# A two-layer transformer stack on one core: 72 identity products on a constant left out in the last third

## The chip, the core and the metric

One core of a Trainium2 chip. The time is the device time of one execution in microseconds (us). The engines are TensorE (PE: matrix products, with its weight loads shown as PEld), VectorE (DVE), ScalarE (ACT), GpSimd (POOL) and the DMA queues; SyncE (SP) issues most of the DMAs. Each engine works through its own list in order, and the lists wait for each other by semaphores.

## What is computed

Batch 2, 1024 tokens, 64 channels, f32. Five steps, each but the first added to its input and behind a layer norm:

```
h = W[x] + pe                                  # embedding and positions
h = h + linear_attention(layernorm(h))         # 8 heads, elu + 1
h = h + moe_block(layernorm(h))                # causal attention, then 8 experts, top 2
h = h + gated_toeplitz(layernorm(h))           # layer 1, the last third of the time
h = h + (layernorm(h) @ weight.T + bias)       # the end
```

The step in the last third, for x = layernorm(h) (the **third norm**):

```
u = silu(x @ u_w.T + u_b);  v = silu(x @ v_w.T + v_b)      # 192 columns each
out = irfft(rfft(a) * rfft(v))[:n]                         # a: a small network of the position
out = (u * out) @ o_w.T + o_b                              # output projection
x_r = silu(srms((x - out) @ t_w.T + t_b));  result = x + x_r
```

Then the **fourth norm** and the last projection (64 to 64 columns).

## The kernel before

All activations stay in SBUF: `h`, `xc`, `sq` and `x1` hold 8 tiles of 128 tokens by 2 x 64 channels (both batches side by side). The order of every engine is written out by hand, one function per engine. PSUM (`ps`) has 8 banks of 128 x 512 f32; which bank a step takes is fixed in the code.

A norm goes like this. DVE (`centre`, L1236) adds what the step before left in PSUM to `h` and subtracts the mean, in two halves; ACT squares each half (L983); DVE sums the squares (L1234) and forms the variance (L1245); ACT takes the root (L1143 for the third norm, L1186 for the fourth); DVE forms the reciprocal and scales the two halves (`scale_rows`, L1250), counting the semaphore `n3` or `n4` up by one for each. PE waits for that semaphore and transposes the tiles, four per half, by products with the identity `idt` (`transposes`, L506). ACT copies the first half to `xT`, DVE the second, and the next products read `xT`.

TensorE's list in the last third, in order:

- the last products of the experts (`last_experts_out`), which the third norm needs;
- `keep_warm(22, 6)` at L868;
- the transposes of the third norm (wait for `n3`);
- 8 steps `uv(n)` for v: four f32 products with 64 rows on `xT` and two bf16 products that add the bias, 192 columns each, and ACT's silu behind each step (L1160);
- the forward transform: 12 groups of 8 products on `tu_s`, with the 8 steps `uv` for u between them; DVE and POOL multiply and add;
- the inverse transform on `tk_s`, 4 units, with transposes (L921) and the two halves of the output projection;
- `keep_warm(4, 3)` at L953;
- the transposes of x - out (wait for `d3`, which DVE counts up at L1592 behind each half of the output projection), the products with `t3` (ACT copies one half of `xT`, L975, DVE the other, L1204);
- `keep_warm(46, 7)` at L957, while DVE and ACT work on srms, silu, the sum and the fourth norm;
- the transposes of the fourth norm (wait for `n4`) and the last projection; DVE adds it to `h` in two halves (L1619), each stored by one DMA.

`keep_warm(n, bank)` multiplies a constant, 128 x 512 in bf16, by the identity, n times:

```
def keep_warm(n, bank):
    for _ in range(n):
        mm(ps[:, bank], ident_b, bfc_s[:, 0:512])
```

Both operands lie in SBUF since the start. The products carry no wait and no semaphore, and nobody reads what they leave in the bank. Seven more calls stand earlier in the kernel; they aren't touched.

In the profile an f32 product is shown as two instructions, a bf16 product as one. The line of most products is L299, that of the helper `mm`.

Of the kernel before, what the change touches and what calls it, by code (L numbers as in the profile page):

```python
# [175 lines left out]
def build(nc, idx, emb, pe, wpack, rpack, epack, ident, bfc, rope, tm, tu, tk, out):  # L176
    with ExitStack() as ctx:
# [51 lines left out]
        def plan(region, *parts):  # L229
# [15 lines left out]

        qst, kst, yT, pt = plan(arena, ([2, B * NH, 512], BF16), ([B * NKV, N], BF16), ([4, 512], F32), ([PT_SLOTS, 2, 512], F32))
        _, _, _, pieces_q0, pieces_k, pieces_q1, e_raw = plan(
            arena, ([B * NH, N], BF16), ([B * NKV, N], BF16), ([4, 512], F32),
            ([NTERM, 512], BF16), ([NTERM, 512], BF16), ([NTERM, 512], BF16), ([NSPLIT], F32))
        pieces_q = (pieces_q0, pieces_q1)  # L250

        _, _, rope_s, tm_s = plan(arena, ([B * NH, N], BF16), ([B * NKV, N], BF16), ([2, N], F32), ([2, NM, L], F32))

        fhl, sil, gh, wb, zp_ = plan(arena, ([NT, B, P], F32), ([2, 512], F32), ([GSLOTS, 3, 512], F32),
# [3 lines left out]

        us, vs, osp, prd = plan(arena, ([NT, 384], F32), ([NT, 384], F32), ([NB * NK, 2, 384], F32), ([4, 2, 384], F32))
        _, yT3 = plan(arena, ([NT, 384], F32), ([NT, 3, P], F32))  # L260

        gt2 = sb("gt2", [P, P])
# [30 lines left out]
        def S(name):  # L293
            if name not in names:
                names[name] = sem(name)
            return names[name]

        def mm(o, l, r, start=True, stop=True, **kw):
            return nc.tensor.matmul(o, l, r, start=start, stop=stop, **kw)  # L299
# [200 lines left out]
        def _(pe):  # L500
            def transposes(src, banks, ready, done, values=(1, 2)):

                for j in range(NT):
                    if j % 4 == 0:
                        pe.wait_ge(ready, values[j // 4])
                    ins = nc.tensor.transpose(ps[:, banks + j // 4, (j % 4) * P:(j % 4 + 1) * P],  # L506
                                              src[:, j].rearrange("p b c -> p (b c)"), idt[:])
                    if j % 4 == 3:
                        ins.then_inc(done, 1)
# [10 lines left out]
# [4 lines that stand above are left out]
# [341 lines left out]
                    ins.then_inc(S("wT"), 1)  # L865
            last_experts_out()

            keep_warm(22, 6)  # L868
            transposes(x1, 2, S("n3"), S("T3"))


# [53 lines left out]
            def output_projection(blk):  # L925

                pe.wait_ge(S("yT3"), 2 * NU * (blk + 1))
                pe.wait_ge(S("uv_silu"), 2 * NT)
                for jj in range(4):
                    n = 2 * (2 * blk + jj - 2) if jj >= 2 else 2 * (2 * blk + 1 - jj) + 1  # L930
                    for c in range(3):
                        ins = mm(ps[:, 6 + blk, jj * P:(jj + 1) * P], yT3[:, n, c, :], W("o3", c * P, (c + 1) * P),
                                 start=(c == 0), stop=(c == 2))
                ins.then_inc(S("o3"), 1)
# [15 lines left out]
            output_projection(0)  # L950
            back_transposes(NB * NU - 1)
            output_projection(1)
            keep_warm(4, 3)  # L953
            transposes(xc, 4, S("d3"), S("T3b"))
            projection("xT3b", "t3", 0, S("t3"))

            keep_warm(46, 7)  # L957
            transposes(sq, 2, S("n4"), S("T4"))
            projection("xT4", "w4", 4, S("o4"))

# [830 lines left out]
```

## Time and profile before

| | before |
|---|---|
| median of 3 runs | 367.31 us (366.73 to 368.72) |
| the profiled execution | 368.48 us, of which the span in the profile 366.7 us |
| mean granted TensorE clock in it | 0.977 of 2.4 GHz |
| PE busy | 323.0 us (88%), 1703 products |
| DVE, ACT, POOL busy | 237.2, 144.1, 105.4 us |
| products with operands in `bfc_s` alone, from 256 us on | 72, 16.0 us busy, mean 379 ns |

The span is cut into 40 slices on the page; the line of PE's busy tenths shows 9 in nearly all slices behind the first eighth, and that of the granted clock 9 in nearly all of them. Three views carry the working: the chain of work that ended last in order of time (what released what), the timeline of a short stretch (what each engine did, with the idle time ahead of it and who ended it), and the table of stretches (busy time of each engine and the granted clock, 1.00 being 2.4 GHz and 0.50 being 1.2 GHz). An instruction's duration includes the time until its result has left the array, so products that follow each other closely overlap, and the sum of their durations is more than the time they take together.

### The profile page before, as it was taken

The page shows a single profiled execution, that of the slowest core. Times are in us where ns is not written, and L with a number is a line of the kernel's source. Part 1 is how long each engine was busy: PE and PEld are TensorE (multiplying, and loading weights), DVE is VectorE, ACT ScalarE, POOL GpSimd, SP SyncE. Part 2 cuts the span into 40 slices and gives each one's busy share as a digit, 9 for nine tenths or more (in the row PEclk, how much of TensorE's full clock was granted, in tenths as well). Part 3 has the DMA queues.
Part 4 walks back from the last instruction along what each step waited for, and adds up shares of the span by engine and source line. Part 5 has one row for each costly group of instructions (what it writes and reads, how often), then busy time and mean ns, then how long its engine had stood idle before and what let it go on. Part 6 is the DMA issues. An engine that isn't in the chain of part 4 may idle for free.

```text
span 366.7 us, 4601 instructions
## 1 busy us (share of the span) xinstructions
PE 323.0 (88%) x1703; PEld 180.6 (49%) x1703; DVE 237.2 (65%) x398; ACT 144.1 (39%) x238; POOL 105.4 (29%) x137
## 2 busy tenths in 40 slices
PE   1256988987999999979999999999999999899995
PEld 0122665552433434656754555555555555467734
DVE  0578678878998740357784555553856677745385
ACT  2022416460586686521554445553450120012250
POOL 5787000236321223200002422221004878700000
PEclk9997899999999999989899999999999999999998
DMA  7939500068000000000000000000000000000001
GB/s 257 321 103 419 216 2 0 0 118 143 2 3 0 4 2 1 2 0 2 0 1 2 0 0 3 0 0 2 1 2 0 0 2 0 0 0 3 0 0 59
DMA packets 6168, 15.29 MB, mean 42 GB/s; under 512 B 1282, under 2 KB 3714, under 8 KB 5506
## 3 DMA queue, kind: packets, MB, share of 16 engines
q1 hardware_dynamic: 5583, 14.45, 12.8%
q0 software_dynamic: 512, 0.53, 0.6%
q8 instruction: 14, 0.23, 0.3%
q14 instruction: 8, 0.07, 0.1%
q10 hardware_dynamic: 51, 0.01, 0.0%
HBM read 12.05 MB, written 0.52 MB: 34 GB/s over the span
## 4 chain that ended last, share of the span: by engine, by line
PE 66%; DVE 15%; ACT 6%; POOL 5%; issue 4%; DMA 2%; SPq 1%; DVEq 0%; POOLq 0%; ACTq 0%
PE ps L299 64%; POOL e_lo L426 2%; DVE arena L1485 1%; DMA idt<-ident 1%; DMA arena<-arena 1%; DVE share L1278 1%; DVE xc L1242 1%; DVE st L1234 1%; DVE st L1241 1%; DVE sq L1250 1%; POOL arena L492 1%; DVE rw L1416 1%; ACT L989 1%; PE ps L506 1%; ACT sq L983 1%
## 5 line engine op out<-in xcount | busy, mean ns | idle before, releaser
L1416 DVE TENSOR_REDUCE rw<-ps 128x1 f32<-128x512 f32 (+2 forms) x80 | 45.7, 629 | 7.6 <-PE ps L299 7.2
L299 PE MATMUL ps<-bfc_s 128*128 128x512 bf16 (+2 forms) x201 | 49.2, 358 | 0.0
L1102 ACT ACTIVATE arena<-ps 128x1024 f32<-128x1024 f32 (+3 forms) x48 | 37.6, 812 | 29.0 <-PE ps L299 28.6
L299 PE MATMUL ps<-arena 96*128 96x512 bf16 (+7 forms) x192 | 43.0, 328 | 1.4 <-DMA arena<-arena 0.8
L299 PE MATMUL ps<-xs,e_hi 128*128 128x512 f32 x96 | 40.6, 423 | 0.6 <-ACT arena L1128 0.6
L1485 DVE TENSOR_TENSOR arena<-ps,arena 128x512 f32<-128x512 f32 x48 | 33.1, 691 | 11.2 <-ACT arena L1128 10.8
L1128 ACT ACTIVATE arena<-ps 128x512 f32<-128x512 f32 x48 | 28.6, 597 | 26.3 <-PE ps L299 22.6
L299 PE MATMUL ps<-xs,e_lo 128*128 128x512 f32 x96 | 38.6, 402 | 0.0
L299 PE MATMUL ps<-share,tu_s 128*128 128x384 f32 x96 | 32.5, 488 | 0.0
L299 PEld LDWEIGHTS ps<-arena 96*128 96x128 bf16 (+1 forms) x192 | 15.8, 98 | 29.0 <-DVE rw L1416 13.2
L299 PEld LDWEIGHTS ps<-bfc_s 128*128 128x128 bf16 x201 | 20.2, 101 | 17.9 <-issue 2.5
L299 PE MATMUL ps<-w,xT 128*128 128x128 f32 (+3 forms) x160 | 26.7, 353 | 2.2 <-DVE xT L1448 0.8
L299 PEld LDWEIGHTS ps<-xs,e_hi 128*128 128x128 f32 x96 | 18.4, 191 | 16.3 <-ACT arena L1128 7.0
L299 PE MATMUL ps<-share,rp 128*128 128x256 f32 x14 | 8.0, 671 | 19.8 <-DVE share L1273 8.4
L299 PEld LDWEIGHTS ps<-w,xT 128*128 128x128 f32 (+1 forms) x160 | 20.0, 210 | 9.5 <-issue 4.8
L458 POOL TENSOR_SCALAR_AFFINE_SELECT arena<-arena 128x256 f32<-128x256 f32 (+1 forms) x32 | 13.8, 433 | 37.1 <-ACT arena L1102 36.6
L299 PE MATMUL ps<-arena,ew 64*64 64x512 f32 (+1 forms) x128 | 24.2, 610 | 0.0
L1264 DVE TENSOR_TENSOR arena<-ps,arena 128x512 f32<-128x512 f32 x16 | 10.3, 687 | 21.0 <-PE ps L299 21.0
L299 PE MATMUL ps<-arena,tk_s 128*128 128x384 f32 x64 | 21.4, 488 | 1.8 <-DVE arena L1555 1.8
L299 PEld LDWEIGHTS ps<-share,tu_s 128*128 128x128 f32 x96 | 17.6, 190 | 10.6
L299 PE MATMUL ps<-arena,va 128*32 128x512 f32 (+3 forms) x192 | 21.6, 505 | 0.7 <-ACT arena L1089 0.5
L299 PEld LDWEIGHTS ps<-xs,e_lo 128*128 128x128 f32 x96 | 18.5, 193 | 2.5
(237 smaller groups left out, 491.5 us busy)
## 6 DMA issues: line engine op xcount, KB each, us to landing
arena<-arena SPq DMA_DIRECT2D x24, 96.0 KB, 2.8
w<-wpack SPq DMA_DIRECT2D x1, 2152.5 KB
arena<-tm SPq DMA_DIRECT2D x2, 1024.0 KB, 5.8
arena<-epack SPq DMA_DIRECT2D x1, 1540.0 KB, 11.4
arena<-rope SPq DMA_DIRECT2D x1, 1024.0 KB
tu_s<-tu SPq DMA_DIRECT2D x2, 512.0 KB, 12.4
tk_s<-tk SPq DMA_DIRECT2D x2, 512.0 KB, 13.9
rp<-rpack SPq DMA_DIRECT2D x1, 678.5 KB, 4.5
```

The costliest lines, as they stand in the source:

```text
L299: return nc.tensor.matmul(o, l, r, start=start, stop=stop, **kw)
L426: nc.gpsimd.tensor_tensor(e_lo[:, 0:E_CUT], e_raw[:, 0:E_CUT], e_hi[:, 0:E_CUT].bitcast(F32), ALU.subtract).then_inc(S("e_split"), 1)
L458: nc.gpsimd.affine_select(out=v, in_=v, pattern=[[0, 2], [1, P + behind]], compare_op=ALU.is_ge, fill=0.0, base=-behind, channel_multiplie ...
L492: nc.gpsimd.tensor_tensor(dst[:, 0], p1[:, 0], p1[:, 1], ALU.subtract).then_inc(S("part"), 1)
L506: ins = nc.tensor.transpose(ps[:, banks + j // 4, (j % 4) * P:(j % 4 + 1) * P], src[:, j].rearrange("p b c -> p (b c)"), idt[:])
L983: nc.scalar.activation(sq[:, 4 * a:4 * a + 4], src[:, 4 * a:4 * a + 4], ACT.Square).then_inc(S("squared"), 1)
L989: nc.scalar.activation(unused[:, loads[0]:loads[0] + 1], idt[0:1, 0:1], func)
L1102: nc.scalar.activation(pt[:, n % PT_SLOTS, :, lo:512], ps[:, bank:bank + 2, lo:512], ACT.Exp, scale=HD ** -0.5).then_inc(S("exp_done"), 1)
L1128: nc.scalar.activation(sil[:, m % 2], ps[:, m % 2], ACT.Silu).then_inc(S("silu"), 1)
L1264: V.tensor_tensor(zp_[:, n % 2], ps[:, 5 + n % 2], wb[:, n % 2], ALU.mult).then_inc(S("zpair"), 1)
L1416: V.tensor_reduce(top_view(m, part)[:, at:at + len(heads), i], src, AXX, ALU.max, negate=True).then_inc(S("ring_read"), 1)
L1485: V.tensor_tensor(gh[:, n % GSLOTS, n3], ps[:, 2 + m % 3], sil[:, m % 2], ALU.mult).then_inc(S("gated"), 1)
```

## The change

The three calls in TensorE's list behind the experts are left out: 22, 4 and 46 products, 72 in all. Nothing is added, no wait is changed, and no other engine's list is touched.

```diff
@@ -865,7 +865,6 @@
             last_experts_out()
 
-            keep_warm(22, 6)
             transposes(x1, 2, S("n3"), S("T3"))
@@ -950,11 +949,9 @@
             output_projection(1)
-            keep_warm(4, 3)
             transposes(xc, 4, S("d3"), S("T3b"))
             projection("xT3b", "t3", 0, S("t3"))
 
-            keep_warm(46, 7)
             transposes(sq, 2, S("n4"), S("T4"))
             projection("xT4", "w4", 4, S("o4"))
```

## Rows read from the trace of the kernel before

**Rows 1.** The page: busy time of PE, and the chain by engine.
```profile
PE 323.0 (88%) x1703; PEld 180.6 (49%) x1703; DVE 237.2 (65%) x398; ACT 144.1 (39%) x238; POOL 105.4 (29%) x137
...
PE 66%; DVE 15%; ACT 6%; POOL 5%; issue 4%; DMA 2%; SPq 1%; DVEq 0%; POOLq 0%; ACTq 0%
```

**Rows 2.** Chain in order, third norm: start us, us, what.
```profile
265.24 0.67 PE ps L506 x4
...
266.72 6.46 PE ps L299 x48
...
273.74 29.92 PE ps L299 x120
```

**Rows 3.** Timeline, third norm: start us, us, engine, line, operation, [idle before].
```profile
257.66 1.97 PE L299 MATMUL ps<-ew,arena 128*128 128x64 f32 x16
...
259.46 4.91 PE L299 MATMUL ps<-bfc_s 128*128 128x512 bf16 x22
...
265.24 1.26 PE L506 MATMUL ps<-idt,x 128*128 128x128 f32 x8 [0.86 <-DVE x L1250]
```

**Rows 4.** Chain piece, then timeline, around the output projection.
```profile
340.00 3.81 PE ps L299 x28
...
342.79 1.03 PE L299 MATMUL ps<-bfc_s 128*128 128x512 bf16 x4
342.99 0.69 DVE L1592 TENSOR_TENSOR xc<-xc,ps 128x512 f32<-128x512 f32 x1 [3.54 <-PE ps L299]
...
343.65 1.04 PE L506 MATMUL ps<-idt,xc 128*128 128x128 f32 x8
344.29 0.58 ACT L975 COPY xT<-ps 128x512 f32<-128x512 f32 x1 [4.33 <-PE ps L506]
344.72 0.69 DVE L1204 COPY xT<-ps 128x512 f32<-128x512 f32 x1 [1.05 <-PE ps L506]
...
344.93 2.05 PE L299 MATMUL ps<-w,xT 128*128 128x128 f32 x16 [0.24 <-ACT xT L975]
```

**Rows 5.** Timeline around the fourth norm and the last projection.
```profile
346.81 10.09 PE L299 MATMUL ps<-bfc_s 128*128 128x512 bf16 x46
...
358.85 1.26 PE L506 MATMUL ps<-idt,sq 128*128 128x128 f32 x8 [1.94 <-DVE sq L1250]
...
360.18 3.36 PE L299 MATMUL ps<-w,xT 128*128 128x128 f32 x16
```

**Rows 6.** Stretches, us: PE, PEld, DVE, ACT, POOL busy (x), PEclk, DMA, GB/s.
```profile
32.99:36.40 3.41, 2.58 (x6) 1.00 (x5) 2.88 (x4) 1.11 (x2) 1.90 (x3) 0.50 0.98 416
36.40:39.82 3.42, 3.42 (x8) 2.01 (x8) 1.57 (x3) 0.35 (x1) 0.00 (x0) 0.50 1.01 414
...
155.90:159.28 3.38, 1.68 (x14) 1.33 (x13) 1.50 (x5) 0.91 (x3) 0.00 (x0) 1.00 0.00 0
159.28:162.70 3.42, 3.28 (x12) 2.39 (x13) 1.25 (x3) 0.45 (x1) 0.00 (x0) 0.50 0.00 0
...
172.90:176.35 3.45, 3.45 (x28) 3.27 (x28) 0.95 (x3) 0.21 (x1) 0.00 (x0) 1.00 0.00 0
176.35:179.76 3.41, 2.99 (x8) 1.87 (x7) 2.59 (x8) 2.54 (x5) 0.00 (x0) 0.50 0.00 0
...
357.25:360.66 3.41, 1.74 (x12) 1.32 (x13) 2.31 (x6) 0.80 (x2) 0.00 (x0) 1.00 0.02 5
360.66:364.07 3.41, 2.88 (x15) 2.58 (x13) 2.49 (x4) 0.00 (x0) 0.00 (x0) 0.50 0.15 56
```

**Rows 7.** Timeline, PE alone: transposes, then products of 128 columns, low clock.
```profile
37.87 0.42 PE L544 MATMUL ps<-idt,share 128*128 128x128 f32 x1
38.08 0.42 PE L545 MATMUL ps<-idt,share 128*128 128x128 f32 x1
...
159.42 2.08 PE L299 MATMUL ps<-w,xT 128*128 128x128 f32 x8 [0.79 <-DVE xT L1448]
```

**Rows 8.** Timeline, PE alone: a long wait without a fall.
```profile
89.04 0.24 PE L299 MATMUL ps<-bfc_s,mpc 128*48 128x128 bf16 x1 [2.19 <-POOL mpc L446]
```

## The prediction

> **What bounds the kernel now.** I read the page first. PE is busy 323.0 of 366.7 us, and the chain that ended last lies on PE for 66% of the span [rows 1]; but a busy share counts the identity products too, so it can't say what they are worth. The chain in order of time can. Around each of the three places the reader should ask one thing: is the PE work there on the chain, or does the chain run over DVE and ACT while PE does something that nobody waits for?
>
> At the third norm (257 to 265 us) the chain runs through DVE and ACT: adding the experts' result, centring, squares, sums, root, scaling. It meets PE again only with the first transposes at 265.24, for 0.67 us, then the two ACT copies and 6.46 us of u and v products [rows 2]. The 22 products of L868 lie beside that, from 259.46 for 4.91 us, so they end at 264.37, before the scaled rows are there; PE then stands idle 0.86 us waiting for DVE [rows 3]. From 273.74 on the chain stays on PE, so what the u and v products lose isn't made up later [rows 2].
>
> At the output projection (340 to 347 us) the 4 products of L953 are on the chain: the piece at 340.00 has 28 products, 24 of the projection and 4 of the identity [rows 4].
>
> At the fourth norm (347 to 359 us) the chain is on DVE and ACT again, and the 46 products (10.09 us from 346.81, so to 356.90) lie beside it; PE then waits 1.94 us for DVE [rows 5].
>
> So two of the three groups cost nothing as work. What they do instead is keep TensorE occupied through 5.6 and 11.9 us in which it would stand still. The granted clock by stretch shows what standing still does here: 1.00 (2.4 GHz) nearly everywhere, 0.50 (1.2 GHz) in four low stretches, of 6.8 us (33 to 40, two rows), 3.4 us from 159.28, 3.4 us from 176.35 and 3.4 us from 360.66 [rows 6]. Ahead of the second and the last, PE was busy for only 1.68 and 1.74 us of the 3.4 us shown; ahead of the third it was full, and the clock fell nevertheless, so the busy share alone doesn't decide. The last one matters most: it came in spite of the 46 products, after 1.94 us of idleness and the transposes, and the final projection is run mostly in it.
>
> **First place (L868, 22 products).** As work: 0, it is hidden by the DVE and ACT work of the norm. That leaves PE idle from the end of the experts' last transposing products (257.66 + 1.97 = 259.63) to 265.24 [rows 3], 5.6 us. That is far more than the 1.94 us ahead of the last low stretch, so I take the clock to be at 1.2 GHz when the transposes start. Costs:
> - Four transposes on the chain. At full clock they take 0.67 us [rows 2]. At half clock one takes 0.42 us and the next starts 0.21 later (37.87 and 38.08) [rows 7]: 0.42 + 3 x 0.21 = 1.05, so +0.4. The other four are covered by the two ACT copies.
> - u and v products until the clock is back. The first eight steps are 48 products (each step 4 on `xT` in f32 and 2 bias products in bf16) in 6.46 us, 0.81 each, one piece of PE in the chain, so PE sets the pace [rows 2]. No row shows it at half clock. Nearest rows: the last projection's 128-column products, 16 in 2.05 us (0.128 each) at full clock [rows 4] against 15 begun or ended in 2.88 us (0.19; 0.23 from start to start below, in the third place) in the low stretch [rows 6], factors 1.5 and 1.8; the two levels give 2 at most. I take 1.75, since these products have more columns (192), and it is columns that the clock counts: each low microsecond loses 0.43. How long? The low stretches lasted 3.4 us where PE was dense and 6.8 us where the first half had holes [rows 6]. Here the front part is used up by idleness and transposes, so the u and v products see between 2.6 and 6 us of it; I take 4.5. Loss 2.0 us, with ends 2.6 x 0.33 = 0.9 and 6 x 0.5 = 3.0. All of it is on the chain.
>
> The Trainium skill (TensorE: Matmul & The Clock Gate, Part 1: The HAM clock gate) says that the array is throttled by default and that activity releases it, and puts the penalty at the throttled time times (1 - K/N). By it 4.5 us at half rate would cost 2.25 us where I take 2.0, an estimate from that page; it speaks against leaving the products out. Its section on PE-mode transpose adds that transposes don't count as busy in the same way; the last low stretch, which fell after eight of them, agrees.
>
> **Second place (L953, 4 products).** The first four transposes need the first half of DVE's subtraction, done at 339.45 (342.99 less the 3.54 that DVE was idle before the second half), so only the 4 products hold them to 343.65. Without these they can start about 342.8, right behind the projection, and the ACT copy about 343.4 instead of 344.29. The second four wait for 342.99 + 0.69 = 343.68 [rows 4]; they end some 0.7 later, the DVE copy at about 345.1 (344.72 + 0.69 = 345.41 before). The projection then starts at about 344.15, runs into that copy at 345.15 for its second half, and ends 1.03 later (8 of its 16 products), near 346.2 instead of 344.93 + 2.05 = 346.98. Gain 0.75 us; its ends are 0.5 and 1.03, the whole duration of the four. What is late next is the second half of the subtraction, hence not 1.03. PE is busy on both sides of this place, so the clock stays.
>
> **Third place (L957, 46 products).** As work: 0, hidden by the DVE and ACT work of the two norms. PE idles 11.9 us before the transposes, so they start at half clock: +0.4 as above. The final projection took 3.36 us for 16 [rows 5]; its first 4 were still at full clock. Entirely low: 8 such products took 2.08 us at 159.42, the last one's drain among it [rows 7]; less that drain some 1.85, 0.23 each from start to start, so 3.5 to 3.8 us: +0.3. Against an execution in which this projection is run at full clock (2.05 us [rows 4]) it is 1.6 instead of 0.3. DVE's and ACT's part isn't changed.
>
> **Sum.** 0.4 + 2.0 - 0.75 + 0.4 + 0.3 = +2.35 us. The profiled execution took 368.48 us (span 366.7 and 1.8 around it), so 370.8. The median of the runs shown is 367.31, 1.2 us less; the runs lie from 366.73 to 368.72. Added to the median, 369.7. But the place of a low stretch can vary between executions, and a median run may well have had its last projection at full clock; then the change costs 2.35 + 1.3 = 3.65 and gives 371.0. I take a value between them, nearer the first: **370.2 us**.
>
> **Rivals.**
> - The clock holds at the first place, or is back before the u and v products. For it: PE idled 2.19 us at 86.7 to 89.0 without the clock falling [rows 8]. Against it: 5.6 us is over twice that. Then -0.75 + 0.7 + up to 1.3: 367.3 to 368.6, not measurable.
> - The other side, faster or no slower: TensorE's clock costs nothing at the end because the granted level doesn't matter to transposes and small products, so only the four products on the chain count. It decides if the last projection's pitch of some 0.2 against 0.128 were not the clock's. Then 367.31 - 0.75 = 366.6. The two pitches at either level speak plainly against it.
> - The clock doesn't come back in the u and v stage. Those products use 64 rows of the array, and no row shows a low stretch ended by such work. The level would then return only in the transform behind 273.74 [rows 2]: 6.46 us of products lose 0.75 to 1.0 of their time, some 5.5 us, plus 1 us of the transform. 367.31 + 0.4 + 6.5 + 0.35 - 0.75 = 373.8.
> - That the change doesn't do what it says: the products write a bank nobody reads before it is overwritten, and no one waits on them; nothing here.
>
> **Chances.** Forecast, 368.7 to 371.8: 0.66. Clock holds or is back early: 0.19. Only the four count: 0.04. Late return: 0.11. The range takes in the forecast and half of either neighbour: 368.2 to 372.0. About 0.5% (1.8 us) is what a measurement of this kernel can tell from no change. Slower by more than that means over 369.15: most of the forecast (0.57) and the late return (0.11), 0.68. Faster by over 0.5% needs more than the four products can give: 0.03. The rest, 0.29, lies between.
>
> **What would show it.** In the profile after: granted clock 0.50 when the transposes at about 265 start and for 2.6 to 6 us of u and v products, whose pitch goes from 0.81 to about 1.4 us; the third-norm chain on DVE unchanged until 264.5; the stretch from the output projection's start (340.00 before) to the last t3 product shorter by 0.75; 0.50 over all of the last transposes and the projection, which takes 3.5 to 3.8 us. The prediction is wrong if the clock is at 1.00 in the u and v stage, if their pitch doesn't follow the clock, or if the low stretch there runs past 273.

## The result and the profile after

The changed kernel takes 375.62 us in the median of 4 runs (374.17 to 376.87), the kernel before 368.01 us (4 runs, 366.73 to 368.79). The ratio is 1.0214, with a 95% interval of 1.0177 to 1.0251: slower by some 7.9 us (7.6 between the two medians). The forecast was 370.2 and a range of 368.2 to 372.0: the direction was right, and the sum of +2.35 us was too small by a factor of more than three.

From the page of the profiled execution (376.05 us, span 374.3): busy time by engine, the granted clock in 40 slices, and the chain by engine.

```profile
PE 314.7 (84%) x1621; PEld 177.9 (48%) x1631; DVE 237.7 (63%) x398; ACT 144.1 (38%) x238; POOL 105.6 (28%) x137
...
PEclk9998999996999999998999999999557999999956
...
PE 66%; DVE 15%; ACT 5%; POOL 5%; issue 5%; DMA 2%; SPq 1%; DVEq 0%; POOLq 0%; ACTq 0%
```

PE is busy for 8.3 us less than in [rows 1], and the kernel takes 7.6 us more of span. The clock line has a hole of 5, 5, 7 in slices 29 to 31, and another near the end. PE's share of the chain is the same 66%: the time went into products that were on the chain anyway.

The 6 in slice 10 lies in code that is the same in both kernels, and up to 264 us the two executions are level within 0.3 us. It is worth a look even so, because it is the wait of [rows 8], 2.20 us here against 2.19 there. Timeline, then stretches (columns as in [rows 6]; the clock is the third number from the end):

```profile
87.45 0.30 PE L299 MATMUL ps<-bfc_s,mpc 128*48 128x128 bf16 x1 [2.20 <-POOL mpc L446]
```

```profile
87.00:90.50 3.50, 3.05 (x8) 1.15 (x9) 2.13 (x4) 0.00 (x0) 0.32 (x2) 0.51 0.57 101
90.50:93.90 3.40, 3.40 (x13) 1.62 (x12) 2.27 (x5) 0.00 (x0) 0.00 (x0) 0.50 0.00 0
```

In this execution the clock fell in that wait and was back at 93.9; in the profiled execution of the kernel before it didn't fall. So whether an idle stretch of 2.2 us costs the clock differs here between executions of the same code. The products that brought it back were dense, bf16, and on 96 and 128 rows in turn.

The chain in order of time (start us, us, what), first around the third norm, then from the output projection to the end:

```profile
264.94 1.97 PE ps L506 x8
266.91 11.06 PE ps L299 x48
...
278.54 33.06 PE ps L299 x120
...
347.96 2.96 PE ps L299 x24
...
351.68 0.66 PE ps L506 x4
352.34 1.96 PE ps L299 x16
...
366.15 1.97 PE ps L506 x8
368.12 3.02 PE ps L299 x16
```

Beside [rows 2], [rows 4] and [rows 5], in us:

| stretch | before | after | difference |
|---|---|---|---|
| start of the third norm's transposes to the first u and v product | 265.24 to 266.72 | 264.94 to 266.91 | +0.5 |
| the first 48 u and v products | 6.46 | 11.06 | +4.6 |
| the next 120, the forward transform | 29.92 | 33.06 | +3.1 |
| output projection to the last t3 product | 340.00 to 346.98 | 347.96 to 354.30 | -0.6 |
| start of the last transposes to the end of the projection | 358.85 to 363.54 | 366.15 to 371.14 | +0.3 |

Together +7.9; the rest up to the 7.6 of the spans lies ahead of 264 us, where the code is the same.

Why the u and v products take 1.7 times as long is seen in the timeline of their first steps, to be held against the 0.81 us per step worked out from [rows 2]:

```profile
266.88 1.01 PE L299 MATMUL ps<-w,xT 64*128 64x192 f32 x4
...
268.26 1.01 PE L299 MATMUL ps<-w,xT 64*128 64x192 f32 x4
```

A step now starts every 1.38 us (266.88, 268.26). The table of stretches gives the level of the clock:

```profile
260.86:264.90 4.04, 0.00 (x0) 0.00 (x0) 3.48 (x8) 1.85 (x3) 0.00 (x0) 0.53 0.00 0
264.90:284.70 19.80, 19.18 (x70) 10.25 (x71) 7.28 (x13) 5.54 (x13) 0.00 (x0) 0.50 0.00 1
284.80:290.00 5.20, 5.20 (x20) 2.83 (x19) 3.65 (x4) 0.49 (x1) 2.29 (x3) 0.98 0.00 0
...
356.40:370.05 13.65, 3.90 (x18) 3.68 (x19) 10.83 (x20) 6.29 (x11) 0.00 (x0) 0.51 0.00 0
```

It is at 0.50 from the idle time ahead of the transposes until about 285.0, 23.9 us in all (the first stretch is cut 0.3 us ahead of the fall, hence 0.53, the third 0.2 us ahead of the return, hence 0.98). That takes in all of the u and v products, in which PE is fully busy, and 6.5 us of the transform: a first `uv` step for u of 1.2 us, then 5.2 us of the transform's own products, which use 128 rows. The last row is the low stretch at the end, with PE idle or in the transposes for most of it. It ended at about 370.3, 0.8 us before the last projection did, which is why that place costs so little here.

### The profile page after: what moved, and what is told of

Its sections match the earlier page's. It is cut to its first block, busy times and chain, and to the rows that moved or that the text cites. A ratio compares the mean times of both kernels' runs of the same rounds, so it can differ in the third digit from the quotient of the medians.

```text
span 374.3 us, 4447 instructions
## 1 busy us (share of the span) xinstructions
PE 314.7 (84%) x1621; PEld 177.9 (48%) x1631; DVE 237.7 (63%) x398; ACT 144.1 (38%) x238; POOL 105.6 (28%) x137
## 4 chain that ended last, share of the span: by engine, by line
PE 66%; DVE 15%; ACT 5%; POOL 5%; issue 5%; DMA 2%; SPq 1%; DVEq 0%; POOLq 0%; ACTq 0%
PE ps L299 64%; POOL e_lo L426 1%; PE ps L506 1%; DVE arena L1482 1%; DMA idt<-ident 1%; DMA arena<-arena 1%; DVE share L1275 1%; DVE xc L1239 1%; DVE st L1231 1%; DVE st L1238 1%; DVE sq L1247 1%; POOL arena L492 1%; DVE rw L1413 1%; ACT L986 1%; ACT sq L980 1%
## 5 line engine op out<-in xcount | busy, mean ns | idle before, releaser
L299 PE MATMUL ps<-arena 96*128 96x512 bf16 (+7 forms) x192 | 44.6, 337 | 1.8 <-DMA arena<-arena 1.0
L299 PE MATMUL ps<-share,tu_s 128*128 128x384 f32 x96 | 35.1, 519 | 0.0
L299 PE MATMUL ps<-bfc_s 128*128 128x512 bf16 (+2 forms) x125 | 33.4, 355 | 0.2
L299 PE MATMUL ps<-w,xT 128*128 128x128 f32 (+3 forms) x160 | 28.6, 389 | 1.7 <-DVE xT L1445 0.8
L299 PEld LDWEIGHTS ps<-share,tu_s 128*128 128x128 f32 x96 | 18.9, 204 | 12.0 <-issue 2.4
L492 POOL TENSOR_TENSOR arena<-arena 128x384 f32<-128x384 f32 x8 | 10.1, 1268 | 40.0 <-DVE arena L1566 40.0
L1157 ACT ACTIVATE arena<-ps 128x384 f32<-128x384 f32 x16 | 7.8, 490 | 34.9 <-PE ps L299 34.9
```

The costliest lines, as they stand in the source:

```text
L492: nc.gpsimd.tensor_tensor(dst[:, 0], p1[:, 0], p1[:, 1], ALU.subtract).then_inc(S("part"), 1)
L1157: nc.scalar.activation(dst.rearrange("p (b c) -> p b c", b=B), ps[:, bank:bank + 2, 0:D1], ACT.Silu).then_inc(S("uv_silu"), 1)
```

## The experiments

Each was run beside the kernel before on the same chip. The first question was which place has the loss, the second why the clock stayed low, the third what each other group is worth.

**Only the 22 left out.**

```diff
-            keep_warm(22, 6)
             transposes(x1, 2, S("n3"), S("T3"))
```

> Only the 22 products ahead of the third norm's transposes are left out; the 4 and the 46 stay. Theory (nearly the whole loss lies here, because the u and v products don't bring the clock back): granted clock 0.50 from about 261 to 285 us, 11 us for the first 48 u and v products instead of 6.5, +8 us against the kernel before. Rival (the three places share the loss, or low stretches elsewhere make it up): +2 to +4 us.

Measured: 374.39 us in the median, ratio 1.0188 (1.0136 to 1.0239). The chain in order of time:

```profile
264.01 1.97 PE ps L506 x8
265.98 11.06 PE ps L299 x48
...
277.60 32.78 PE ps L299 x120
```

By the ratio +6.9 us. The same 1.97, 11.06 and nearly the same 32.78 us as in the changed kernel: the loss lies in this place.

**The rest of the change, without it.** The changed kernel with the 22 put back, so the 4 and the 46 are left out.

```diff
-            keep_warm(4, 3)
...
-            keep_warm(46, 7)
```

> The changed kernel with the 22 products put back, so only the 4 and the 46 are left out. Theory (the loss of the change is the first place's alone): -0.75 from the 4 and +0.3 to +1.0 from the 46, so within 0.5 us of before, some 7.5 us faster than the changed kernel; no low stretch between 260 and 345 us. Rival (the places depend on each other): +2 us or more.

Measured over 12 runs: 368.68 us, ratio 1.0010 (0.9984 to 1.0036). Chain:

```profile
266.25 6.46 PE ps L299 x48
...
273.28 29.92 PE ps L299 x120
...
359.73 3.62 PE ps L299 x16
```

6.46 and 29.92 us are the figures of before, to the hundredth. The two other groups together make no difference that can be told from none, so the two experiments add up to the change: 1.0188 and 1.0010 against 1.0214.

**128 rows instead of 64 in the u and v products, nothing to hold the clock.** The low stretches of the kernel before had been ended by products on all 128 rows of the array; the f32 products for u and v use 64, one batch each. (The weights are already stored with zeros outside each batch's block, so only the slices change. The two bias products of a step use 96 rows in both kernels.)

```diff
-                    mm(ps[:, bank + b, 0:D1], xT[64 * b:64 * b + 64, at:at + P],
-                       W(("v3", "u3")[n // NT], b * D1, (b + 1) * D1)[64 * b:64 * b + 64],
-                       start=True, stop=False, tile_position=(64 * b, 0), skip_group_check=True)
+                    mm(ps[:, bank + b, 0:D1], xT[:, at:at + P],
+                       W(("v3", "u3")[n // NT], b * D1, (b + 1) * D1),
+                       start=True, stop=False, skip_group_check=True)
```

> The changed kernel (all 72 left out), but each f32 product of the u and v steps uses all 128 rows of the array: the weights are stored with zeros outside their batch's block, so the whole 128 rows of xT and of the weights can be taken, with the same 192 columns and the same number of instructions. Theory (a product on 64 rows isn't enough activity to bring the clock back): the clock is back at 1.00 within 3.4 to 6.8 us of the u and v products' start at 267, before 274; 3 to 5 us faster than the changed kernel, +3 to +5 against before. Rival (the rows don't matter, it is the columns or the bf16 products between them): low until about 285 as in the changed kernel, +7.5 us or more.

Measured over 10 runs: 369.65 us (367.81 to 373.16), ratio 1.0052 (1.0014 to 1.0090): 6 us of the 7.9 are back, with none of the 72 products in the kernel. The chain, and then the stretches:

```profile
263.15 1.97 PE ps L506 x8
265.12 7.63 PE ps L299 x48
...
273.32 30.27 PE ps L299 x120
```

```profile
259.60:263.10 3.50, 0.00 (x0) 0.00 (x0) 2.98 (x7) 1.85 (x3) 0.00 (x0) 0.50 0.00 0
263.10:266.40 3.30, 3.25 (x12) 2.84 (x13) 1.35 (x3) 1.13 (x4) 0.00 (x0) 0.50 0.00 0
266.40:270.00 3.60, 3.60 (x27) 3.26 (x26) 1.12 (x3) 1.96 (x4) 0.00 (x0) 0.99 0.00 0
```

The clock fell as before, ahead of the transposes, but was back at 266.4, one step into the u and v products; 7.63 us for the 48 instead of 11.06, and a transform at full pace. The times fall into two groups, six at 367.8 to 369.9 and four at 371.5 to 373.2, so the return probably comes later in some executions. The mean granted clock fits that without proving it (0.953 to 0.962 in the six, 0.944 to 0.954 in the four); only one of the first group was profiled.

**The same edit with all 72 in place**, for what it costs by itself.

> The kernel before with the same edit of the u and v products (128 rows instead of 64), all 72 identity products kept: what the edit costs by itself. Both theories: the two products of one step can no longer overlap in different rows of the array, so a step may take 0.80 to 0.97 us instead of 0.81; 16 steps, 0 to +2.5 us against before, clock 1.00 throughout the stage.

Measured over 10 runs: 368.81 us, ratio 1.0026 (0.9996 to 1.0056). Chain:

```profile
264.56 6.99 PE ps L299 x48
...
272.12 30.27 PE ps L299 x120
```

6.99 us instead of 6.46: at full clock the wider products cost 0.5 us for eight steps, so the gain above isn't that they are cheaper.

**The 22 products on 64 rows.** If a clock that is up needs all rows to stay up, this should drop it although PE is as busy as before.

```diff
-            keep_warm(22, 6)
+            for _ in range(22):
+                mm(ps[:, 6], ident_b[0:64], bfc_s[0:64, 0:512], tile_position=(0, 0), skip_group_check=True)
```

> The kernel before with the 22 identity products at the third norm done on 64 rows of the array instead of 128 (same 512 columns, same number; the 4 and the 46 unchanged). Theory (the monitor wants rows as well as columns): the clock falls although PE is as busy as before, low from 262 or 265 until the transform, +6 to +8 us against before. Rival (any busy array counts): no low stretch at 260 to 285, +0 us.

Measured over 10 runs: 368.49 us, ratio 1.0025 (0.9999 to 1.0051). The theory as I had put it fell. The timeline and the stretches:

```profile
258.67 4.92 PE L299 MATMUL ps<-bfc_s 64*128 64x512 bf16 x22
```

```profile
258.00:263.80 5.80, 5.59 (x29) 2.59 (x28) 5.17 (x10) 1.99 (x4) 0.00 (x0) 1.00 0.00 0
263.80:273.00 9.20, 7.85 (x58) 4.33 (x60) 5.09 (x11) 5.55 (x12) 0.00 (x0) 1.00 0.01 2
```

Here work on 64 rows held a clock that was up: 1.00 throughout. That agrees with a thing I should have read in the kernel before, whose u and v products on 64 rows ran at full clock all the time. Left was a narrower theory: such work holds the clock but doesn't bring it back.

**A burst behind the transposes, on 64 rows and on 128.** Two kernels, both the changed one with 24 products of 512 columns between the transposes and the u and v products; they lengthen the kernel, and only the clock was of interest.

```diff
             transposes(x1, 2, S("n3"), S("T3"))
+            for _ in range(24):
+                mm(ps[:, 6], ident_b[0:64], bfc_s[0:64, 0:512], tile_position=(0, 0), skip_group_check=True)
```

> The changed kernel with a burst of 24 identity products of 512 columns between the third norm's transposes and the u and v products, done on 64 rows of the array. It lengthens the kernel; only the clock is read. Theory (work on 64 rows can hold a clock that is up, but can't bring it back): every product of the burst starts 0.43 us behind the one before, some 10 us in all, and the clock stays at 0.50 through the u and v products until the transform. Rival (columns back to back are what brings it back, and the u and v products only lack those): back at 1.00 within the burst.

> The same burst of 24 products on all 128 rows. Theory and rival both: the clock is back at 1.00 within 3.4 to 6.9 us of the burst's start, the burst takes some 7 to 9 us, and the u and v products behind it have the pitch of before, 0.81 us, since they hold a clock that is up.

On 64 rows, one run of 385.19 us; the burst in the timeline (the last of the 24 falls between the first u and v products), and the stretches:

```profile
266.83 9.99 PE L299 MATMUL ps<-bfc_s 64*128 64x512 bf16 x23
```

```profile
267.00:277.00 10.00, 10.00 (x26) 3.87 (x25) 0.69 (x2) 0.00 (x0) 0.00 (x0) 0.50 0.00 0
277.00:288.00 11.00, 10.95 (x48) 4.92 (x45) 3.08 (x6) 3.45 (x8) 0.00 (x0) 0.50 0.01 1
```

23 products in 9.99 us, 0.43 each, without a hole, and the clock stays at 0.50, through 10 us of the burst and 11 of the u and v products. On 128 rows, one run of 376.97 us; the first part of the burst in the timeline, then the stretches:

```profile
268.15 4.05 PE L299 MATMUL ps<-bfc_s 128*128 128x512 bf16 x9
```

```profile
268.30:272.20 3.90, 3.90 (x10) 1.37 (x10) 0.76 (x2) 0.00 (x0) 0.00 (x0) 0.50 0.00 0
272.20:275.00 2.80, 2.62 (x13) 1.20 (x13) 0.00 (x0) 0.00 (x0) 0.00 (x0) 0.98 0.00 0
275.00:282.00 7.00, 6.94 (x51) 3.39 (x49) 3.08 (x6) 3.46 (x8) 0.00 (x0) 1.00 0.01 2
```

The burst starts at 268.15 and the clock is back at about 272.3, after 4.2 us of it, and stays up through the u and v products. The two kernels differ in the rows, and in one thing that came with them: the products on 64 rows name their part of the array (`tile_position`), those on 128 don't. The edit of the u and v products changed both as well, and no run separates them. Each burst was run once. With that said, in every trace taken here products on 64 rows kept a clock that was up and never brought back one that was down.

**How many products, and where.** 11 instead of 22 at the front of the gap:

```diff
-            keep_warm(22, 6)
+            keep_warm(11, 6)
```

> 11 instead of 22 products at the third norm, so PE is idle for some 3.3 us more ahead of the transposes. If any activity in part of the gap holds the clock: +0 us. If what counts is how long PE stands idle just ahead of the transposes: low from the transposes on and until the transform, +6 to +8 us, perhaps not in every execution. No number is favoured.

Four executions of 369.85, 370.02, 375.35 and 377.56 us. The profiled one has the low stretch; timeline and stretch:

```profile
266.26 1.97 PE L506 MATMUL ps<-idt,x 128*128 128x128 f32 x8 [3.23 <-DVE x L1250]
```

```profile
265.20:285.00 19.80, 18.16 (x69) 9.59 (x70) 8.24 (x15) 6.54 (x13) 0.00 (x0) 0.50 0.00 1
```

3.23 us of idleness ahead of the transposes were enough in this one. The times say the same of the 375.35 us execution and the opposite of the two near 370, and the mean granted clock agrees: 0.954 and 0.959 in the long ones, 0.972 in both short ones. With two such groups the median (372.69) says little. Then 10 products at the end of the gap:

```diff
-            keep_warm(22, 6)
+            pe.wait_ge(S("squared"), 8)
+            keep_warm(10, 6)
```

> 10 instead of 22 products at the third norm, and moved to the end of the gap by a wait for the second half of the squares (about 262.9): PE is idle for 3.3 us first and then busy until just ahead of the transposes. The kernel with 11 at the front of the gap had two executions near 370 and two at 375 to 378. If the position decides: always near before, +0 to +0.5 us. If only the amount within some stretch counts: low in some executions and not in others here too, +0 or +8 us, two groups of times.

Measured over 12 runs: 369.75 us, all from 368.29 to 370.31, ratio 1.0041 (1.0020 to 1.0062). Timeline and stretches:

```profile
261.01 4.45 PE L299 MATMUL ps<-bfc_s 128*128 128x512 bf16 x10 [3.35 <-ACT sq L984]
```

```profile
262.00:266.00 4.00, 4.00 (x13) 1.89 (x11) 1.55 (x3) 1.69 (x3) 0.00 (x0) 0.50 0.00 0
266.00:275.00 9.00, 8.17 (x61) 4.61 (x60) 4.69 (x10) 4.57 (x10) 0.00 (x0) 0.97 0.00 0
```

Not what either expectation said. The clock did fall in the gap, the ten products run at half pace (4.45 us), and by 266.5 it is back: they didn't hold the clock, it came back behind them, during the transposes and just in time for the u and v products. The cost is 1.5 us by the ratio. The ten themselves can account for it: they end at 265.46, some 2.3 us after DVE has scaled the first half (about 263.2), and the transposes wait for them. All 12 executions are on the good side.

**Only the 4 left out.**

```diff
-            keep_warm(4, 3)
             transposes(xc, 4, S("d3"), S("T3b"))
```

> Only the 4 products between the output projection and the t3 transposes are left out. Theory (they are on the chain): -0.75 us, the stretch from the second half of the output projection to the last t3 product 6.4 us instead of 7.0, no low stretch there. Rival (the short gap costs the clock): 0 or more.

Measured: 366.76 us over 6 runs, ratio 0.9977 (0.9940 to 1.0013). Chain:

```profile
339.26 2.96 PE ps L299 x24
...
342.99 0.66 PE ps L506 x4
343.64 1.96 PE ps L299 x16
```

339.26 to 343.64 + 1.96 = 345.60, 6.34 us, against 340.00 to 346.98 in [rows 4]: 0.64 us gained in the profile. In the times -0.85, an interval that reaches zero.

**Only the 46 left out.**

```diff
-            keep_warm(46, 7)
             transposes(sq, 2, S("n4"), S("T4"))
```

> Only the 46 products ahead of the fourth norm's transposes are left out. Theory (they buy little, since the last projection lies in a low stretch even with them): the eight transposes take 1.97 us instead of 1.3, the projection 2.9 to 3.7; +0.3 to +1.0 us. Rival (they hold the clock in most runs of before, and the profiled run is an unlucky one): +1.5 to +2 us.

Measured: 368.83 us over 6 runs, ratio 1.0022 (0.9991 to 1.0053), inconclusive by itself. Chain:

```profile
359.20 1.97 PE ps L506 x8
361.17 3.18 PE ps L299 x16
```

1.97 + 3.18 = 5.15 us against 4.69 in the profile of before: 0.46 us for 46 products. But that profile had its last projection mostly in a low stretch, and not every execution has. Of the eight profiled kernels that keep the 46 products at this place or put 53 there, three have it low (3.36 us in [rows 5], 3.46 with the 128-row u and v products, 3.58 with the 22 on 64 rows) and five at full clock, the kernel without the 4 among them:

```profile
357.45 1.26 PE L506 MATMUL ps<-idt,sq 128*128 128x128 f32 x8 [1.94 <-DVE sq L1249]
358.79 2.05 PE L299 MATMUL ps<-w,xT 128*128 128x128 f32 x16
```

From 357.45 to 360.84 that is 3.39 us. Against such an execution the 46 are worth 1.8 us, so the rival of this run isn't ruled out: the profiled execution of before is one of two kinds. The times, +0.8 us by the ratio with an interval from -0.3 to +2.0, lie between.

**A version to keep.** Without the 4, and with the two hidden groups made as long as their gaps.

```diff
-            keep_warm(22, 6)
+            keep_warm(25, 6)
...
-            keep_warm(4, 3)
...
-            keep_warm(46, 7)
+            keep_warm(53, 7)
```

> The 4 on the chain left out, and the two hidden groups made long enough to fill the gap in which PE waits: 25 instead of 22, 53 instead of 46. Theory: -0.75 us from the first, 0 to -1.3 us from the last projection run less in a low stretch: -0.7 to -1.5 us in the median. Rival (the last low stretch comes from the transposes and not from the idle time): -0.75 and no more.

Measured: 366.41 us over 6 runs beside 367.61 of before, ratio 0.9951 (0.9920 to 0.9982), 1.8 us faster by it (1.2 between the medians), and faster than both kernels. Timeline:

```profile
259.30 5.56 PE L299 MATMUL ps<-bfc_s 128*128 128x512 bf16 x25
...
346.00 11.60 PE L299 MATMUL ps<-bfc_s 128*128 128x512 bf16 x53
358.03 1.26 PE L506 MATMUL ps<-idt,sq 128*128 128x128 f32 x8 [0.43 <-DVE sq L1249]
359.36 2.05 PE L299 MATMUL ps<-w,xT 128*128 128x128 f32 x16
```

The groups end at 264.86 and 357.60, just ahead of the transposes, and the last projection takes 2.05 us, the full-clock figure, instead of 3.36 in [rows 5]. That the longer groups did this isn't shown: the kernel without the 4 has the same 2.05 us with 46 products and 1.94 us of idleness, and its median of 366.76 us can't be told from 366.41. What is shown is that the version as a whole is faster than before.

## Why the prediction was wrong

Point by point:

- **What is hidden and what is on the chain**: right. The 22 and the 46 cost nothing as work, the 4 did. The chain on DVE and ACT up to the scaled rows of the third norm didn't change.
- **The clock falls at the first place**: right. It was at 0.50 before the transposes, 0.5 us more until the first u and v product where 0.4 was expected.
- **What a low microsecond costs**: right. The factor was taken as 1.75; 11.06 / 6.46 is 1.71, on products for which no row had it.
- **How long it lasts**: wrong, and this is the step that failed. "The low stretches lasted 3.4 us where PE was dense and 6.8 us where the first half had holes", so 4.5 us of the u and v products were taken, 6 at most. The low stretch lasted 23.9 us by the profile, all 11.06 us of those products and 6.5 of the transform. The inference went from the work that had ended the four low stretches in the trace (all of it on 128 rows) to f32 work on 64 rows that was just as dense. The term was 2.0 us with an end at 3.0; it measured 4.6 in the u and v products and 3.1 in the transform.
- **The rival that came true**: "The clock doesn't come back in the u and v stage", with a chance of 0.11. Its reason, 64 rows, held up, as far as the bursts can show. Even so it was priced too low, at 373.8: its transform was given 1 us, and 3.1 were lost, because 5.2 us of dense 128-row work passed at half pace before the clock was back. (In the burst it was 4.2 us, and with the 64-row burst ahead of the transform 2.3: the clock was at 0.50 from 289.76, where the transform's own products begin, to 292.0.) With 3.1 in its place it would have read 375.9, near the measured median partly by luck: its 5.5 us for the u and v products were 4.6, and it took 0.35 for the third place where the sum has 0.7. Given that no row showed such work ending a low stretch, 0.11 was too little, and the range should have reached that rival.
- **Second place**: expected -0.75, measured -0.64 in the profiles.
- **The rival that the clock holds**: it rested on [rows 8], a wait of 2.19 us (from 86.85, not 86.7) without a fall. The same wait did cost the clock in the changed kernel's execution, so that row was no support. No trace shows the clock holding through the 5.6 us.
- **Third place**: expected +0.7 against the profiled execution, measured +0.3 there, +0.46 with the 46 alone left out. The transposes cost 0.64 more until the projection starts (1.33 to 1.97); the projection gained 0.35, because the low stretch happened to end in it. The guess that many executions of before have this projection at full clock was sound, as the other profiles show, and against those the place costs more.

The Trainium skill (TensorE: Matmul & The Clock Gate, Terms) prices throttled time at (1 - K/N) of it, K/N being the granted share, 0.50 here. From the transposes at 264.94 to 285.0 that is half of 20.1, an estimate of 10 us; the three terms measured together 8.2, the u and v products having slowed by 1.71 and not by 2. The trace agrees with it as an upper bound. Its Part 4: PE-mode transpose says that transposes don't count as busy in the same way. The prediction saw the last low stretch agree, but the kernel without the 4 ran the same eight transposes behind the same 1.94 us of idleness without a fall in them or in the projection. And with 128 rows in the u and v products the clock returned at 266.4, 3.3 us after the first transpose, of which the transposes were the first 2.0. That speaks against it, as one profile can; no run here separates transposes from other products.

Not settled: whether it is the rows as such, the product of rows and columns in use, or the naming of a part of the array. Nor where between 64 and 128 rows the difference lies: the low stretch at 87 us ended under products on 96 and 128 rows in turn, while the u and v products, of which two in six use 96, didn't end theirs. Fewer columns on 128 rows, dense, were not tried in a low stretch. And it isn't known why the runs with 128-row products fall into two groups.

## What to carry to other kernels

Idle-time filler isn't judged by how the engine is occupied, but by what comes after the gap: find the first dense work behind it, and ask whether that work brings the clock back, or only holds it. Here 22 hidden products were worth 7 us because products on half the array's rows came next, and 46 were worth 0.5 to 1.8 us, by the execution, because only 16 products did. Filler on the chain costs its time, 0.64 us for the four here, so let it end before the work that it precedes is ready. If the fill is to be short, 10 products at the end of the gap did better than 11 at its front. And one profile isn't enough to price a clock effect: the same code had the clock up in one execution and down in the next.

## What the runs showed of the hardware that was not expected

- Dense products on 64 rows, 23 of 512 columns in 9.99 us and 48 more in 11 us, left the granted clock at 0.50; the same burst on 128 rows had it back at 1.00 after 4.2 us (one run each).
- The same 64-row products held it at 1.00: 22 in 4.92 us, and the u and v products of the kernel before.
- Behind ten 128-row products at half pace at the end of a gap (4.45 us) the clock was back at about 266.5, in the transposes that followed; all 12 times lay within 2.1 us.
- With 11 products at the front of the gap, the same program took 370 us in two executions and 375 to 378 in two. There is no sharp edge at this 3.2 us: a wait of 2.2 us in unchanged code cost the clock in one kernel's execution and not in another's, and behind 1.94 us of idleness the last projection was low in three profiles and at full clock in four.
